# A megakernel of four stages: clearing a finished stage's semaphores on SyncE inside the next stage, and the sum and two norms ahead of the latent attention as one block

## The chip, the cores and the metric

One core of one Trainium2 chip runs the whole program. The metric is the device time of one execution in microseconds, taken as the median of several runs. A profiled execution gives the trace on which the working rests.

## What is computed

The input is x, 2048 tokens of 128 features. Four residual sublayers follow each other, each closed by a layer norm without weights:

```python
x = _layernorm(x + mamba_block(x))             # state space, 4 heads
x = _layernorm(x + local_transformer(x))       # two layers: 8 heads, window 64, gated feed-forward
x = _layernorm(x + latent_attention(x))        # 16 heads; begins with a layer norm of its own input
x = _layernorm(x + experts(x))                 # 16 experts, 4 per token, and a shared one

def _layernorm(x, axis=-1, eps=1e-05):
    m = jnp.mean(x, axis=axis, keepdims=True)
    v = jnp.var(x, axis=axis, keepdims=True)
    return (x - m) / jnp.sqrt(v + eps)
```

The latent attention starts with `h = (x - mu) * rsqrt(var + eps) * ln_scale + ln_bias`, so between the local transformer and the latent attention a sum and two norms stand in a row: `x + y`, the norm of the sublayer, and the norm of its result without the weights (the weights are put on after the transposes).

## The kernel before

The tokens lie in 16 tiles of 128 (T = 16), the partitions hold the tokens of a tile and the free dimension the 128 features; four tiles make a chunk of 512 (NC = 4). x_tok and y_tok are two such arrays of [128, 16, 128] that stay in SBUF through the whole kernel, in float32.

The program is a row of blocks (`nc.Block()`). In a block each engine has its own list of instructions, and the engines are ordered among each other by semaphores; at a block's end all engines meet at a barrier. Between two blocks nothing overlaps. `Space` (L34) holds the tiles and the semaphores of a stage, and notes every semaphore it hands out in `Space.used`. Semaphores count upwards, so one must be back at zero before its number is used anew. `clear_semaphores` (L63) does that: a block of its own in which GpSimd clears every used semaphore one by one (L70), after which they are released. It is called four times: after the state space and its two norms (L522; 49 semaphores), after each of the two layers of the local transformer (L1198; 56 and 55), and after the latent attention and its norm n2 (L1792; 64).

`normalise` (L76) is a block: for each of 16 tiles the vector engine takes statistics (L93) and aggregates them (L96); ScalarE takes the root of all 16 variances at once (L128), the vector engine inverts it (L101) and normalises tile by tile (L105). The last output of it is needed by the next block.

The local transformer (L1168) begins with a small block in which SyncE issues four loads: the weights wqkv and rows of layer 0 (L539, L540), the mask band (L1183) and the rotation tables turns (2 MB, L1184). The vector engine waits for band, casts it, and with that the block ends. Then each layer (`attention_layer`, L543) runs three blocks: the projections (`project_qkv`, L555), the windowed attention and the feed-forward. In the projections' block SyncE loads wo (L593) and waits for it. TensorE transposes the tokens in four groups (L603), projects q, k (L614) and v (L618) tile by tile, and transposes the rotated result (L630); ScalarE copies one half of each transposed group (L650) and squares q and k (L656); the vector engine copies the other half (L695), rotates (L703, L711) and sums the squares (L718); GpSimd first scales the rotation tables (L749, it needs turns) and then adds (L756) and scales (L762) each tile. TensorE takes up the first two groups, then tile 0, group 2, tile 1 and group 3, in this order.

After layer 1 and its clearing a block with a single instruction adds the two arrays (L1203, 2048 columns), then come `normalise` n1 (L1204) and, inside `latent_attention` (L1221), `normalise` gn (L1232), which writes to the other array. The next block (ga, L1245) issues its loads of weights, transposes and projects. The main part of the latent attention is a loop of four turns over heads and chunks; the change does not touch it. The experts' first block (L1833) issues seven loads on SyncE (L1838, L1840).

## Time and profile before

| | |
|---|---|
| median of 3 runs | 2432.08 us (2427.37 to 2432.56) |
| the profiled execution | 2424.45 us |
| its span | 2422.6 us |
| TensorE busy | 2123.5 us (88%) |
| TensorE weight loads busy | 1305.8 us (54%) |
| vector engine busy | 1629.8 us (67%) |
| ScalarE busy | 1383.3 us (57%) |
| GpSimd busy | 900.5 us (37%) |
| DMA moved | 345.62 MB |

The profile is of one execution. A busy TensorE counts the time in which a matmul is under way, whatever the clock; the clock granted to it is shown beside it, where 1.00 is 2.4 GHz and 0.50 is 1.2 GHz. Names ending in q (SPq, POOLq) are the instructions that an engine's queue carries out itself: issuing a DMA, setting, waiting for or clearing semaphores, and draining at a barrier. They are not counted as busy. SP is SyncE, POOL is GpSimd, DVE is the vector engine, ACT is ScalarE, PE is TensorE, PEld its weight loads. A row of the timeline gives the start, the duration, the engine and line, the operation with output<-input, the shapes, how many instructions were merged, and in brackets how long the engine had been idle and what released it. Times of the trace count from the start of the span.

### The profile page before, as it was taken

Reading aid. Unit: us, or ns where it says so; the run is one execution under the profiler, and the core shown is the slowest. Engines: PE = TensorE matmul, PEld = TensorE weight load, DVE = VectorE, ACT = ScalarE, POOL = GpSimd, SP = SyncE. Lnnn points to the kernel's source line nnn. Section 1 sums busy time; section 2 is a strip of 40 time slices with the busy share of each in tenths; the row PEclk is TensorE's granted clock in tenths of the full one; section 3 lists DMA queues with packets and bytes.
Section 4 is the critical chain, followed back from the end, with each engine's and each line's share of the span. In section 5 each row is a group of like instructions: output and inputs, shape, how many; then the busy total and the mean of one; then the engine's idle time right before and its main releaser. Section 6 shows DMA issues by size and latency. Waiting matters only on the chain. (4 is left out here: it accounts for less than half of the span.)

```text
span 2422.6 us, 38119 instructions
## 1 busy us (share of the span) xinstructions
PE 2123.5 (88%) x11662; PEld 1305.8 (54%) x11662; DVE 1629.8 (67%) x3035; ACT 1383.3 (57%) x2804; POOL 900.5 (37%) x889
## 2 busy tenths in 40 slices
PE   4745898889964799999999999999999999996497
PEld 2533486547742455555555555555555555553254
DVE  5767765576655677777677776777776777773544
ACT  4333665366520477777677776777776777773121
POOL 0635632474302334444344343443434434442000
PEclk8887899989986799999999999999999999998598
DMA  1001000000004476767677676677766776673100
GB/s 32 1 1 58 1 2 27 5 1 2 2 12 153 132 235 231 242 230 240 207 232 241 231 239 232 218 232 238 231 231 219 239 232 233 228 242 123 36 1 18
DMA packets 224395, 345.62 MB, mean 143 GB/s; under 512 B 16992, under 2 KB 169696, under 8 KB 223904
## 3 DMA queue, kind: packets, MB, share of 16 engines
q1 hardware_dynamic: 224160, 342.86, 42.9%
q8 instruction: 102, 1.67, 0.3%
q14 instruction: 133, 1.09, 0.1%
HBM read 148.55 MB, written 136.31 MB: 118 GB/s over the span
## 5 line engine op out<-in xcount | busy, mean ns | idle before, releaser
L1503 DVE TENSOR_REDUCE g.most<-g_score 128x1 f32<-128x512 f32 x1028 | 639.5, 684 | 350.5 <-PE g_score L1473 347.9
L1511 ACT ACTIVATE g.probs<-g_score,g.bias 128x1024 f32<-128x1024 f32 x514 | 568.6, 1111 | 67.1 <-DVE g.bias L1506 55.7
L1473 PE MATMUL g_score<-g.keys,g.q_unit 128*128 128x512 f32 x2056 | 561.2, 413 | 25.4 <-DMA g.q_unit<-g.q_pair 11.8
L1496 ACT ACTIVATE g.near<-g_turned 128x512 f32<-128x512 f32 x512 | 305.4, 597 | 322.1 <-PE g_turned L1492 322.1
L1473 PEld LDWEIGHTS g_score<-g.keys,g.q_unit 128*128 128x128 f32 x2056 | 360.7, 190 | 145.0 <-ACT g.probs L1511 61.8
L1492 PEld LDWEIGHTS g_turned<-top.ident,g.probs 128*128 128x128 f32 x2048 | 234.1, 140 | 243.0 <-issue 208.1
L1570 DVE STREAM_TRANSPOSE g.blocks<-g.probs 128x1024 f32<-128x1024 f32 x256 | 318.9, 1246 | 23.9 <-DMA bounce<-g.blocks 16.2
L1492 PE MATMUL g_turned<-top.ident,g.probs 128*128 128x128 f32 x2048 | 321.6, 279 | 0.0
L1524 PE MATMUL g_mix_ps<-g.near,mid.y_tok 128*64 128x512 f32 x1056 | 258.7, 611 | 6.6 <-DMA g.far<-bounce 6.6
L1524 PE MATMUL g_mix_ps<-g.far,mid.y_tok 128*64 128x512 f32 x1056 | 255.2, 605 | 0.0
L1590 POOL TENSOR_TENSOR mid.y_tok<-mid.y_tok,g.waves 128x512 f32<-128x512 f32 x128 | 164.3, 1284 | 231.9 <-ACT mid.y_tok L1488 231.9
L1552 POOL TENSOR_TENSOR g.scaled<-g.scaled,g.recip 128x512 f32<-128x512 f32 x67 | 69.8, 1042 | 425.9 <-ACT g.scaled L1544 414.8
L1524 PEld LDWEIGHTS g_mix_ps<-g.near,mid.y_tok 128*64 128x64 f32 x1056 | 64.9, 137 | 104.9 <-issue 97.0
L1524 PEld LDWEIGHTS g_mix_ps<-g.far,mid.y_tok 128*64 128x64 f32 x1056 | 64.3, 136 | 99.5 <-issue 99.5
L1511 ACT ACTIVATION_READ_ACCUMULATOR g.probs<-g_score,g.bias 128x1 f32 x514 | 100.5, 195 | 0.0
L1601 POOL TENSOR_TENSOR g.k_part<-mid.y_tok,g.zero 128x256 fp32r<-128x256 f32 x64 | 39.3, 613 | 155.9 <-DMA g.keys<-g.k_part 150.7
L1593 POOL TENSOR_TENSOR mid.y_tok<-mid.y_tok 128x256 f32<-128x256 f32 x128 | 93.5, 730 | 10.0
L1556 POOL TENSOR_TENSOR top.x_tok<-top.x_tok,g.scaled 128x512 f32<-128x512 f32 x67 | 85.8, 1280 | 5.2
L1488 ACT ACTIVATE mid.y_tok<-g_side 128x512 f32<-128x512 f32 x128 | 77.4, 605 | 2.0
L881 POOL TENSOR_TENSOR lt0.probs<-lt0.probs,lt0.total 128x768 f32<-128x768 f32 x32 | 47.0, 1468 | 71.3 <-DVE lt0.total L936 71.3
L881 POOL TENSOR_TENSOR lt1.probs<-lt1.probs,lt1.total 128x768 f32<-128x768 f32 x32 | 47.0, 1468 | 71.2 <-DVE lt1.total L936 71.2
L1349 PE MATMUL g_side<-g.c,g.w_up 64*128 64x256 f32 x512 | 72.6, 402 | 0.0
(362 smaller groups left out, 3184.9 us busy)
## 6 DMA issues: line engine op xcount, KB each, us to landing
bounce<-g.blocks SPq DMA_DIRECT2D x256, 512.0 KB, 5.2
g.far<-bounce SPq DMA_DIRECT2D x256, 512.0 KB, 4.4
g.q_unit<-g.q_pair SPq DMA_DIRECT2D x132, 256.0 KB, 4.7
g.keys<-g.k_part SPq DMA_DIRECT2D x256, 64.0 KB, 3.5
g.far<-g.near SPq DMA_DIRECT2D x8, 512.0 KB, 5.8
lt.turns<-turns SPq DMA_DIRECT2D x1, 2048.0 KB, 9.1
g.waves<-g_waves SPq DMA_DIRECT2D x1, 2048.0 KB, 10.2
g.keys<-g.probs SPq DMA_DIRECT2D x16, 128.0 KB, 2.3
```

The lines of the kernel that those rows point to most:

```text
L881: nc.gpsimd.tensor_tensor(p, p, total[:, slot].unsqueeze(2).broadcast_to([P, HH, KEYS]), ALU.mult).then_inc(m["probs_ready"], 1)
L1473: ins = nc.tensor.matmul(score[:, b], q[:, part], k_of(b), start=(part == 0), stop=(part == 1))
L1488: nc.scalar.activation(raw[:, kind], side[:, kind], ACT.Copy).then_inc(m["piece_taken"], 1)
L1492: ins = nc.tensor.transpose(turned[:, k * P:(k + 1) * P], probs[:, r % 2, t * P:(t + 1) * P], ident[:])
L1496: nc.scalar.activation(near[:, w, tiles, r * P:(r + 1) * P], turned[:].rearrange("p (t n) -> p t n", n=P), ACT.Copy).then_inc(m["near_copi ...
L1503: nc.vector.tensor_reduce(most[:, slot, k:k + 1], score[:, k], AX.X, ALU.max, negate=True)\
L1511: nc.scalar.activation(probs[:, slot, k * 2 * CH:(k + 1) * 2 * CH], score[:, 2 * k:2 * k + 2].rearrange("p b n -> p (b n)"), ACT.Exp, bias ...
L1524: ins = nc.tensor.matmul(out, values[:, t], moving, start=(t < 2), stop=(t >= T - 2))
L1556: nc.gpsimd.tensor_tensor(a, a, scaled[:], ALU.add).then_inc(m["added"], 1)
L1570: nc.vector.transpose(blocks[:, r % 2].rearrange("p j t c -> p t j c"), probs[:, r % 2, NEAR * P:].rearrange("p (t j a) -> p t j a", j=4, ...
L1590: nc.gpsimd.tensor_tensor(both, both, waves[:, at].rearrange("p s n -> p (s n)"), ALU.mult)\
L1593: nc.gpsimd.tensor_tensor(total, total, both[:, QH:], ALU.add).then_inc(m["order"], 1)
```

## The change

`clear_semaphores` is gone. `retire_semaphores` only sets the used semaphores aside, with no instruction; `clear_retired` clears them on SyncE, one by one, in a block of the next stage:

- the 49 of the state space in the first block of the local transformer, between the loads of wqkv and rows and the loads of band and turns;
- the 56 of layer 0 in the projections' block of layer 1, between the load of wo and the wait for it;
- the 55 of layer 1 in the new block with the sum and the two norms, where SyncE has nothing else to do;
- those of the latent attention in the experts' first block, behind its seven loads.

The sum, n1 and gn become one block, `normalise_twice`. The sum is cut in four pieces of 512 columns. Statistics, aggregation, root and reciprocal are as before. The mean of a normalised tile is taken as zero and its variance as var / (var + eps), which two multiplications of the 16 variances give (`left`); ScalarE takes a second root, and the vector engine inverts it between its fourth and fifth tile (`again`). The vector engine normalises each tile in place, and ScalarE multiplies each by its value of `again` and writes it to the other array. The array cur takes the second norm, x the first, as before.

```diff
--- before.py
+++ after.py
@@ -35,7 +35,7 @@
-    used = []
+    used, retired = [], []
     def __init__(self, nc, name):
         self.nc, self.name, self.stack = nc, name, ExitStack()
@@ -60,17 +60,17 @@
         return sem
-def clear_semaphores(nc):
-    with nc.Block() as block:
-        @block.gpsimd
-        def _(pool):
-            for _, sem in Space.used:
-                pool.sem_clear(sem)
-    while Space.used:
-        Space.used.pop()[0].__exit__(None, None, None)
+def retire_semaphores():
+    Space.retired, Space.used = Space.used, []
+def clear_retired(sync):
+    for _, sem in Space.retired:
+        sync.sem_clear(sem)
+    while Space.retired:
+        Space.retired.pop()[0].__exit__(None, None, None)
 def normalise(nc, name, src, dst, scale=None, shift=None, residual=None):
@@ -131,6 +131,65 @@
+def normalise_twice(nc, x, cur, after):
+    with Space(nc, "n1") as sp:
+        stats = sp.sb("stats", [P, T, 6])
+        moments = sp.sb("moments", [P, T, 2])
+        spread = sp.sb("spread", [P, T])
+        again = sp.sb("again", [P, T])
+        left = sp.sb("left", [P, T])
+        eps = sp.sb("eps", [P, 1])
+        names = ["eps_ready", "summed", "stats_ready", "std_ready", "order", "left_ready", "left_std", "again_ready",
+                 "once"]
+        m = {n: sp.sem(n) for n in names}
+        with nc.Block() as block:
+            @block.sync
+            def _(sync):
+                after(sync)
+            @block.vector
+            def _(dve):
+                nc.vector.memset(eps[:], EPS).then_inc(m["eps_ready"], 1)
+                for g in range(NC):
+                    tiles = slice(4 * g, 4 * g + 4)
+                    nc.vector.tensor_tensor(x[:, tiles], x[:, tiles], cur[:, tiles], ALU.add).then_inc(m["summed"], 1)
+                for t in range(T):
+                    dve.wait_ge(m["summed"], t // 4 + 1)
+                    nc.vector.bn_stats(stats[:, t], x[:, t]).then_inc(m["order"], 1)
+                for t in range(T):
+                    dve.wait_ge(m["order"], t + 1)
+                    ins = nc.vector.bn_aggr(moments[:, t], stats[:, t])
+                ins.then_inc(m["stats_ready"], 1)
+                dve.wait_ge(m["std_ready"], 1)
+                link = Chain(dve, m["order"])
+                link.n = T
+                link(nc.vector.reciprocal(spread[:], spread[:]))
+                dve.wait_ge(m["stats_ready"], 1)
+                link(nc.vector.tensor_tensor(left[:], moments[:, :, 1], spread[:], ALU.mult))
+                nc.vector.tensor_tensor(left[:], left[:], spread[:], ALU.mult).then_inc(m["left_ready"], 1)
+                for t in range(T):
+                    if t == 4:
+                        dve.wait_ge(m["left_std"], 1)
+                        nc.vector.reciprocal(again[:], again[:]).then_inc(m["again_ready"], 1)
+                    nc.vector.tensor_scalar(x[:, t], x[:, t], moments[:, t, 0:1], spread[:, t:t + 1],
+                                            ALU.subtract, ALU.mult).then_inc(m["once"], 1)
+            @block.scalar
+            def _(act):
+                act.wait_ge(m["eps_ready"], 1)
+                act.wait_ge(m["stats_ready"], 1)
+                nc.scalar.activation(spread[:], moments[:, :, 1], ACT.Sqrt, bias=eps[:, 0:1])\
+                    .then_inc(m["std_ready"], 1)
+                act.wait_ge(m["left_ready"], 1)
+                nc.scalar.activation(again[:], left[:], ACT.Sqrt, bias=eps[:, 0:1]).then_inc(m["left_std"], 1)
+                act.wait_ge(m["again_ready"], 1)
+                for t in range(T):
+                    act.wait_ge(m["once"], t + 1)
+                    nc.scalar.activation(cur[:, t], x[:, t], ACT.Copy, scale=again[:, t:t + 1])
 HEADS_S, HEAD_S, STATE = 4, 64, 128
 INNER = HEADS_S * HEAD_S
 TAPS = 4
@@ -519,7 +578,7 @@
         normalise(nc, "ssn", out_tok, out_tok, ln_w, ln_b, x_tok)
     normalise(nc, "n0", out_tok, out_tok)
-    clear_semaphores(nc)
+    retire_semaphores()
@@ -591,6 +650,8 @@
             @block.sync
             def _(sync):
                 sync.dma_start(wo[:], dram[f"wo{layer}"]).then_inc(m["wo_loaded"], 16)
+                if layer:
+                    clear_retired(sync)
                 sync.wait_ge(m["wo_loaded"], 16)
             @block.tensor
@@ -1180,6 +1241,7 @@
                 @block.sync
                 def _(sync):
                     load_projection(sync, dram, tables, 0)
+                    clear_retired(sync)
                     sync.dma_start(band32[:], dram["band"]).then_inc(got, 16)
                     sync.dma_start(tables["turns"][:], dram["turns"]).then_inc(tables["loaded"], 16)
@@ -1195,13 +1257,8 @@
                     nc.vector.tensor_copy(tables["band"][:], band32[:])
         for layer in range(DEPTH):
             attention_layer(nc, dram, const, tables, layer, x if layer == 0 else cur, cur)
-            clear_semaphores(nc)
-        with nc.Block() as block:
-            @block.vector
-            def _(dve):
-                nc.vector.tensor_tensor(x[:], x[:], cur[:], ALU.add)
-    normalise(nc, "n1", x, x)
+            retire_semaphores()
+        normalise_twice(nc, x, cur, after=clear_retired)
@@ -1229,7 +1286,6 @@
         waves = sp.sb("waves", [P, HALVES, 2, QH])
         mixers = sp.sb("mixers", [P, 2 + HEADS_G, D])
         waves_loaded = sp.sem("waves_loaded")
-        normalise(nc, "gn", x, acc)
         with Space(nc, "ga") as s:
             norm = s.sb("norm", [P, 2])
             w_down = s.sb("w_down", [P, 2 * LATENT])
@@ -1789,7 +1845,7 @@
                 take_output(act, UNITS + 2)
     normalise(nc, "n2", acc, x)
-    clear_semaphores(nc)
+    retire_semaphores()
@@ -1838,6 +1894,7 @@
                         sync.dma_start(d[:], dram[n]).then_inc(m["loaded"], 16)
                     for d, n in ((w_gate, "w_gate"), (w_up, "w_up_e"), (w_down, "w_down_e")):
                         sync.dma_start(d[:], dram[n]).then_inc(w_loaded, 16)
+                    clear_retired(sync)
                 @block.tensor
                 def _(pe):
```

## Rows read from the trace of the kernel before

**Rows 1.** The timeline around the sum and the two norms: start us, us, engine line operation

```profile
710.66 0.29 DVE L1142 TENSOR_TENSOR top.x_tok<-top.x_tok,fp_prod 128x128 f32<-128x128 f32 x1 [0.38 <-PE fp_prod L1054]
...
715.04 2.29 DVE L1203 TENSOR_TENSOR mid.y_tok<-mid.y_tok,top.x_tok 128x2048 f32<-128x2048 f32 x1 [4.09 <-PEq L65]
...
717.67 3.19 DVE L93 BATCH_NORM_STATS2 n1.stats<-mid.y_tok 128x6 f32<-128x128 f32 x16
...
723.65 0.25 DVE L101 RECIPROCAL n1.spread<-n1.spread 128x16 f32<-128x16 f32 x1 [1.72 <-ACT n1.spread L128]
...
737.94 1.94 PE L1259 MATMUL ga_turned<-top.ident,top.x_tok 128*128 128x128 f32 x8 [27.32 <-PEq L87]
```

**Rows 2.** The timeline around the first joint, after the state space

```profile
188.67 4.19 DVE L105 TENSOR_SCALAR mid.y_tok<-mid.y_tok,n0.moments,n0.spread 128x128 f32<-128x128 f32 x16
...
196.51 0.33 SPq L539 DMA_DIRECT2D lt.wqkv<-wqkv  x1
...
197.36 0.42 SPq L1183 DMA_DIRECT2D lc.band<-band  x1
...
202.59 1.94 PE L603 MATMUL lp_turned<-top.ident,mid.y_tok 128*128 128x128 f32 x8 [33.74 <-PEq L1178]
...
207.00 9.30 POOL L749 TENSOR_TENSOR lp0.turns<-lt.turns,lt.rows 128x1024 f32<-128x1024 f32 x4 [10.02 <-DMA lt.turns<-turns]
```

**Rows 3.** The timeline around the joint of layer 0 and layer 1

```profile
454.56 0.29 DVE L1142 TENSOR_TENSOR top.x_tok<-top.x_tok,fp_prod 128x128 f32<-128x128 f32 x1 [0.38 <-PE fp_prod L1054]
...
459.30 1.94 PE L603 MATMUL lp_turned<-top.ident,top.x_tok 128*128 128x128 f32 x8 [4.78 <-PEq L65]
...
460.42 0.70 DVE L695 COPY lp1.hT<-lp_turned 64x512 f32<-64x512 f32 x1 [0.85 <-PE lp_turned L603]
...
465.18 0.60 PE L603 MATMUL lp_turned<-top.ident,top.x_tok 128*128 128x128 f32 x4
...
467.34 1.22 DVE L703 TENSOR_TENSOR lp1.rotated<-lp_qk_ps,lp1.turns 128x1024 f32<-128x1024 f32 x1 [0.76 <-ACT lp1.square L656]
```

**Rows 4.** The timeline around the joint before the experts

```profile
2237.43 4.19 DVE L105 TENSOR_SCALAR mid.y_tok<-top.x_tok,n2.moments,n2.spread 128x128 f32<-128x128 f32 x16
...
2246.23 0.36 SPq L1838 DMA_DIRECT2D ea.router<-router  x1
```

**Rows 5.** Queue instructions of one line: count, ns min/median/max, first and last start us

```profile
L70 POOLq EVENT_SEMAPHORE_RANGE_CLEAR  x49: 37/38/47, 193.1 to 196.2; - x49
...
L65 POOLq EVENT_SEMAPHORE  x8: 17/17/17, 196.3 to 2246.1; - x8
...
L65 SPq EVENT_SEMAPHORE  x4: 17/17/17, 196.4 to 2246.2; - x4
```

**Rows 6.** Timeline, then stretches with TensorE's granted clock (ahead of the DMA share)

```profile
222.92 1.88 PE L614 MATMUL lp_qk_ps<-lt.wqkv,lp0.hT 128*128 128x512 f32 x4
...
408.77 0.67 PE L1026 MATMUL fp_prod<-top.x_tok,lt.moved 128*128 128x256 f32 x2 [0.65 <-PEq L801]
...
408.20:408.75 0.55, 0.00 (x0) 0.01 (x1) 0.25 (x1) 0.02 (x1) 0.01 (x1) 1.00 0.00 0
...
459.20:460.30 1.10, 1.00 (x5) 1.03 (x6) 0.17 (x2) 0.00 (x0) 0.95 (x1) 0.50 0.13 15
```

**Rows 7.** Transfers by issue: count, KB each, us from issue to landing

```profile
la1.wo<-wo SPq DMA_DIRECT2D x1, 256.0 KB, 2.5
...
lc.band<-band SPq DMA_DIRECT2D x1, 192.0 KB, 4.5
```

**Rows 8.** ScalarE's groups of one shape: count | busy us, mean ns | idle before

```profile
L670 ACT ACTIVATE la0.qkT<-lp_turned 128x512 f32<-128x512 f32 x32 | 17.2, 594 | 5.1 <-PE lp_turned L630 5.1
...
L1097 ACT ACTIVATE ff0.gelu<-fp_g_ps,ff0.b 128x512 f32<-128x512 f32 x12 | 8.2, 687 | 23.4 <-PE fp_g_ps L1044 23.4
...
L216 ACT ACTIVATE ss.xbc<-ss.xbc,ss.conv_b 128x2048 f32<-128x2048 f32 x4 | 8.0, 2001 | 14.9 <-DVE ss.xbc L245 14.9
...
L495 ACT ACTIVATE ssd.square<-ss.gate 128x256 f32<-128x256 f32 x16 | 6.7, 416 | 9.1 <-PEq L341 8.7
```

## The prediction

> **What bounds the kernel now.** Read the page from its fourth part first. The chain that ended last is of little use here: it is followed back only through the last norm and stops at a barrier, so its shares of the span are all next to nothing. So the question is not which engine is the bottleneck of the whole span, but what happens on the few stretches that the change touches. These are the joints between stages, so the next view is the timeline around each joint, with the engines' queues: the work on both sides of a joint is serial (a barrier of all engines stands between two blocks), and whatever is taken out of a joint is taken out of the time, unless something that starts with the next block is late anyway.
>
> There are two kinds of joint. A plain one, such as the end of the sum on the vector engine (715.04 + 2.29 = 717.33) to the first statistics at 717.67, costs 0.33 us [rows 1]. One with clearing is long: 188.67 + 4.19 = 192.86 to 196.51 is 3.65 us [rows 2]; 454.85 to 459.30 is 4.45 [rows 3]; 710.95 to 715.04 is 4.09 [rows 1]; 2241.62 to 2246.23 is 4.61 [rows 4]. The row of the clearing line names the cause [rows 5]: 49 clears on GpSimd's queue, the last one 3.1 us after the first, so 64 ns apart though each is 38 ns long. The lists of the other three joints are, counted in the code, 56, 55 and 64 long, and at 64 ns they fill those gaps too. During a clear all other engines wait at the barrier.
>
> **The change, part by part.**
>
> *Layer 0 to layer 1 of the local transformer (56 clears).* The clears go to SyncE behind the load of wo in the first block of layer 1. That block lasts from 459 to past 531, SyncE has nothing else in it, so 56 x 64 ns = 3.6 us are covered; without that cover they would cost themselves. Joint: 4.45 - 0.33 = 4.1 us saved. There is more. The row of the window from 459.2 shows TensorE's granted clock at 0.50 (1.2 GHz) after 4.8 us of idle; the joint at 408.2, where the engine had been idle for 0.65 us, shows 1.00 (2.4 GHz) [rows 6]. With the clears gone the idle time at this joint is about 0.7 us, close to the second case, so I take it that layer 1 starts at 2.4 GHz. What it is worth: before, the third group of transposes starts at 465.18, 5.9 us after the block's first one, and this releases ScalarE's square and then the vector engine's first rotation at 467.34 [rows 3]. At full clock four transposes take 0.6 (half of what 1.94 for eight gives, with the tail), the copy of 0.70 follows, then six matmuls (four for q and k, two for v) at 0.43 each, since four take 1.88 with their tail [rows 6]: 0.65 + 0.75 + 2.6 = 4.0 instead of 5.9. Then the vector engine is the limit of the block, tile after tile, so the 1.8 us stay. Late next is GpSimd, whose scaling of the turns (9.3 us for four pieces) stands before its first addition; but in layer 0 it started only at 207.00, 4.4 us after that block's first transposes, and the block was hardly longer. Sum: **5.9**, bounds 4.1 (clock falls all the same) and 6.3.
>
> *State space to local transformer (49 clears).* Here the clears stand in SyncE's queue between the loads of wqkv and rows and the loads of band and turns. The block opens 3.65 - 0.33 = 3.3 earlier, at 193.2. SyncE needs 197.36 - 196.51 = 0.85 for the two loads ahead [rows 2], then 49 clears. No row shows a clear on SyncE. From above: a DMA issue, 0.42 long and with the same gap 0.45 apart [rows 2]. From below: a semaphore event takes 17 ns on SyncE and 17 ns on GpSimd [rows 5], so the engines are alike there, and with the gap of 26 ns between instructions 43 ns is the floor. The nearest row is the same instruction on GpSimd, so I take 64: 3.1 us, and band is issued at 193.2 + 0.85 + 3.1 = 197.2 instead of 197.36. Nearly the whole gain is eaten by the new place. What is left comes from the transfer: band landed 4.5 us after its issue, behind 0.9 MB of wqkv and rows issued at the same moment; wo of layer 1, larger than band and alone, took 2.5 [rows 7]. With wqkv under way 3.3 us earlier I take 2.7 for band. The vector engine's cast and the barrier are unchanged, so the block after it starts (4.5 - 2.7) + 0.17 = **2.0** earlier. Late next: turns (2 MB), issued right behind band, on which GpSimd waits until 207.00 [rows 2]; they come some 1.5 earlier, and GpSimd had slack there as well. Bounds: 0.2 (landing still takes 4.5) and 3.4 (clears at 43 ns, landing in 2.3); far below zero at the price of a DMA issue, see the rivals. TensorE starts cold here both ways.
>
> *Layer 1, the sum and two norms.* Before: 710.95 (end of the last add) to 737.94 (first transposes of the latent attention), 27.0 us [rows 1]. After: the 55 clears run on SyncE beside the norm, 3.5 us within some 16, and are covered. The block opens at 711.28. The sum in four pieces costs what one did, 2.29, plus the start of three instructions, from 0 to 3 x 0.19 (one of sixteen statistics in 3.19); 0.15 taken: 713.7. From the first statistics to the first reciprocal nothing changes, 723.65 - 717.67 = 6.0 (it contains ScalarE's table load): 719.7. Then come that reciprocal, 0.25, and two small multiplications, at most as long each: 720.5 with rounding up. Sixteen tiles take 4.19 in every norm [rows 2], four of them 1.05: 721.55, then the second reciprocal, 0.3 with its signal: 721.85. The second root on ScalarE runs under the first four tiles. From here ScalarE copies sixteen tiles of 128 columns with a scale read from a column. Its price comes from four rows [rows 8]: 256 columns from SBUF take 0.416, 2048 with a column operand 2.001; a column operand costs 0.687 - 0.594 = 0.093 at 512 columns; so a column of width costs (2.001 - 0.093 - 0.416) / 1792 = 0.83 ns, and a tile 0.416 - 0.107 + 0.093 = 0.40. Back to back they overlap: 32 of 0.594 are busy for only 17.2, in pairs, so 0.11 are hidden. At 0.30 apart, 15 x 0.30 + 0.40 = 4.9: 726.75. The vector engine is done at 725.0, so ScalarE ends the block. With 0.3 of barrier the next one starts at 727.05 instead of 737.94: **10.9**. Bounds 10.3 (no overlap of the small ones, more start cost) and 12.5 (ScalarE keeps up with the vector engine). No work is moved behind the joint: the loads of the latent attention are issued in the next block as before and shift with it.
>
> A rule of the Trainium skill bears on this: Perfetto Trace Analysis, Optimizing Scalar/DVE Operations, advises larger operations, as each has a fixed cost, and gives about 93 ns for ScalarE on SBUF. By it, as an estimate, a tile would come every 0.2 us, ScalarE would stay just behind the vector engine, and this part would give 12.5 instead of 10.9; the same rule speaks against cutting the sum in four, at about 0.06 us for each start. The trace does not bear out the 93 ns as the whole price here: a column operand alone adds as much again [rows 8].
>
> *Latent attention to experts (64 clears before; they go behind the seven loads of a block of some 43 us).* 4.61 - 0.33 = **4.3**. TensorE had long been idle and starts cold both ways. Bounds 4.1 and 4.4.
>
> **The sum.** 2.0 + 5.9 + 10.9 + 4.3 = 23.1 us. The profiled execution took 2424.45 (span 2422.6 and 1.85 around it), so a profile of the changed kernel should read 2401.3. The median of the runs shown is 2432.08, 7.6 above the profiled one and itself in a spread of 5.2; the loop of the latent attention, some 1400 us, is not touched. I predict 2432.1 - 23.1 = **2409.0**.
>
> **The rivals.**
>
> *The clock falls all the same* in layer 1's first block. For it: the granted clock there was 0.50, and I argue from one short joint. Against: that joint. It gives 23.1 - 1.8 = 21.3, so 2410.8.
>
> *ScalarE keeps up* with the vector engine in the joined norm. For it: plain copies without a column operand come 0.2 apart. Against: the 0.093 of a column operand [rows 8]. It gives 24.7, so 2407.4. This is the result of the rule of the Trainium skill cited above, and has the same chance.
>
> *A clear on SyncE is dear.* This is the case on the slow side. SyncE's other work is DMA issues at 0.45 us each; if a clear cost p, the joints would give together 26.2 - 49 p for p up to 0.28 (at 0.064 that is the sum above), and beyond that 55 clears also outlast the 15.5 us of the joined norm, which costs a further 55 (p - 0.28). The gain is zero at p = 0.40; at 0.45 it is 26.2 - 22.0 - 9.4 = -5.2, so 2437. Against: semaphore events take 17 ns on both engines [rows 5].
>
> *The gain is real but other stretches move.* Every cold start of TensorE and the phase of the transfers in the long loop shift by chance; four iterations of that loop at 0.5 us each, and the runs' spread, could take away or add up to 8: 2401 to 2417. Here also falls that the code of a new stage was loaded under the clears: the joint with 56 clears is 0.3 longer than the others' spacing gives.
>
> **Chances.** Forecast 0.62; clock falls 0.11; ScalarE keeps up 0.10; other stretches move 0.13, of which 0.02 hide the gain altogether; dear clears 0.04, of which 0.03 are slower. The range runs from 2401 (all upper bounds, 26.6, and 4.5 of spread) to 2416 (all lower bounds, 18.7, and 2.6), and leaves out less than 2 in 10. A difference of 0.2%, 4.9 us, is about what a measurement of this kernel can tell from none. Faster 0.94, same 0.03, slower 0.03.
>
> **What would show it.** In the changed profile: the clearing rows under SyncE with their spacing (43 to 64 ns right, 400 wrong); the vector engine's gaps at the three other joints near 0.33; the first window of layer 1 at clock 1.00 and the first rotation about 6.2 us after the block's first transpose (8.0 before); band landing some 2.7 us after its issue; ScalarE's sixteen copies 0.30 apart and ending 1.5 us or more after the vector engine's last tile; and some 16 us from the first piece of the sum to the first transpose of the latent attention (22.9 before). The prediction is wrong if SyncE's clears are slow, if band lands as late as before, or if the long loop takes another time than before.

## The result

| | before | after |
|---|---|---|
| median | 2432.32 us (2427.37 to 2433.67, 4 runs) | 2403.61 us (2399.72 to 2404.37, 4 runs) |
| profiled execution | 2424.45 us | 2404.37 us |
| its span | 2422.6 us | 2402.6 us |

After stands to before as 0.9884 (95% interval 0.9867 to 0.9901): 28.7 us faster, between 24.1 and 32.3. The forecast was 2409.0 with a range from 2401 to 2416, so the time fell into the range, 5.4 us below the forecast.

The two profiled executions differ by only 20.0 us. The stretch that makes the difference is the loop of the latent attention, which the change does not touch: measured from the first issue of w_up to the first statistics of n2, it took 1469.5 us in the profile of before and 1475.1 in that of after. Over the 13 traces of this study it took from 1468.6 to 1479.4, and three traces of the kernel before alone read 1469.5, 1475.9 and 1477.2. So here the traces are compared outside that loop, joint by joint: the time outside it is 953.1, 954.2 and 951.5 us in three traces of before, and 927.5 and 929.9 in two of after (the second is the run after_again, below). That is a difference of 24.2 between the means.

The timeline of after at the first joint (start us, us, engine line operation, then the idle time before it and what released it; [rows 2] is its counterpart; the row of L105 is still n0's sixteen tiles):

```profile
189.12 4.19 DVE L105 TENSOR_SCALAR mid.y_tok<-mid.y_tok,n0.moments,n0.spread 128x128 f32<-128x128 f32 x16
...
193.57 0.33 SPq L598 DMA_DIRECT2D lt.wqkv<-wqkv  x1
...
197.79 0.33 SPq L1245 DMA_DIRECT2D lc.band<-band  x1
...
200.81 1.94 PE L664 MATMUL lp_turned<-top.ident,mid.y_tok 128*128 128x128 f32 x8 [31.51 <-PEq L1239]
...
207.68 9.29 POOL L810 TENSOR_TENSOR lp0.turns<-lt.turns,lt.rows 128x1024 f32<-128x1024 f32 x4 [13.63 <-DMA lt.turns<-turns]
...
210.13 1.22 DVE L764 TENSOR_TENSOR lp0.rotated<-lp_qk_ps,lp0.turns 128x1024 f32<-128x1024 f32 x1 [2.22 <-POOL lp0.turns L810]
```

The block opens early (wqkv at 193.57, 0.26 after the norm's end at 193.31; 3.65 before), band is issued 4.5 us after the norm's end, exactly as before, and the first transposes come 7.50 after it instead of 9.73. But the last row is new: the vector engine waits 2.22 us for GpSimd's scaled turns, which begin at 207.68.

The clearing rows of after, by stretch (count: ns min/median/max, first and last start; [rows 5] is the counterpart):

```profile
L71 SPq EVENT_SEMAPHORE_RANGE_CLEAR  x49: 25/30/49, 194.4 to 197.7; - x49
...
L71 SPq EVENT_SEMAPHORE_RANGE_CLEAR  x56: 25/28/30, 454.9 to 458.1; - x56
...
L71 SPq EVENT_SEMAPHORE_RANGE_CLEAR  x55: 25/30/31, 704.9 to 708.5; - x55
...
L71 SPq EVENT_SEMAPHORE_RANGE_CLEAR  x61: 25/25/46, 2232.1 to 2236.0; - x61
```

A clear on SyncE takes 25 to 30 ns, less than GpSimd's 38, yet they come 58 to 69 ns apart (3.3 us over 48 steps in the first row): nearly GpSimd's spacing. So the time of the instruction does not set the spacing; no run shows what does.

The joint of layer 0 and layer 1, timeline of after ([rows 3]):

```profile
454.62 1.06 PE L664 MATMUL lp_turned<-top.ident,top.x_tok 128*128 128x128 f32 x8 [0.65 <-PEq L1059]
...
458.78 0.60 PE L664 MATMUL lp_turned<-top.ident,top.x_tok 128*128 128x128 f32 x4
...
460.95 1.23 DVE L764 TENSOR_TENSOR lp1.rotated<-lp_qk_ps,lp1.turns 128x1024 f32<-128x1024 f32 x1 [0.76 <-ACT lp1.square L717]
```

and the window over its first transposes (window, length, busy time of PE, PEld, DVE, ACT, POOL with their counts, granted clock, DMA share, GB/s; [rows 6]):

```profile
454.60:455.70 1.10, 1.06 (x8) 0.85 (x8) 0.58 (x3) 0.41 (x1) 1.03 (x1) 1.00 0.32 26
```

TensorE was idle for 0.65 us instead of 4.78, the clock stayed at 1.00 (2.4 GHz), eight transposes took 1.06 instead of 1.94, and the first rotation comes 6.3 us after the first transpose instead of 8.0.

The joined norm, timeline of after ([rows 1]; ahead of it the last addition of the block before, then the sum, the reciprocals, the two outputs and the next block):

```profile
704.36 0.29 DVE L1203 TENSOR_TENSOR top.x_tok<-top.x_tok,fp_prod 128x128 f32<-128x128 f32 x1 [0.39 <-PE fp_prod L1115]
...
705.00 2.50 DVE L157 TENSOR_TENSOR mid.y_tok<-mid.y_tok,top.x_tok 128x512 f32<-128x512 f32 x4
...
713.38 0.25 DVE L168 RECIPROCAL n1.spread<-n1.spread 128x16 f32<-128x16 f32 x1 [1.71 <-ACT n1.spread L183]
713.67 0.17 DVE L170 TENSOR_TENSOR n1.left<-n1.moments,n1.spread 128x16 f32<-128x16 f32 x1
713.88 0.17 DVE L171 TENSOR_TENSOR n1.left<-n1.left,n1.spread 128x16 f32<-128x16 f32 x1
...
715.16 3.08 DVE L176 TENSOR_SCALAR mid.y_tok<-mid.y_tok,n1.moments,n1.spread 128x128 f32<-128x128 f32 x12
715.28 4.78 ACT L190 ACTIVATE top.x_tok<-mid.y_tok,n1.again 128x128 f32<-128x128 f32 x16 [0.88 <-DVE n1.again L175]
...
720.35 1.94 PE L1315 MATMUL ga_turned<-top.ident,top.x_tok 128*128 128x128 f32 x8 [16.02 <-PEq L146]
725.26 1.53 DVE L1344 TENSOR_SCALAR ga.hT<-ga_turned,ga.norm 128x512 f32<-128x512 f32 x2 [7.02 <-DMA ga.w_o<-w_o]
```

From the end of the last addition to the first transposes of the latent attention it is now 720.35 - 704.65 = 15.70 us, 26.99 before. The vector engine has its last tile at 718.24, ScalarE its last copy at 720.06: ScalarE ends the block, by 1.8 us. The last row is a wait that the prediction does not name: the vector engine of the next block stands until 725.26, 4.9 us after the first transposes, for the weights. It stood there before as well (6.0 us after them).

The joint before the experts ([rows 4]):

```profile
2224.19 4.19 DVE L105 TENSOR_SCALAR mid.y_tok<-top.x_tok,n2.moments,n2.spread 128x128 f32<-128x128 f32 x16
2228.64 0.95 POOL L1931 MEMSET ea.comb<- 128x1024 f32 x1 [11.26 <-POOLq L87]
2228.64 0.36 SPq L1894 DMA_DIRECT2D ea.router<-router  x1
```

2228.38 to 2228.64 is 0.26, where it was 4.61.

### The profile page after: what moved, and what is told of

Read it like the earlier page. It is cut to its first block and busy times, and to the rows that moved or that the text cites. A ratio compares the mean times of both kernels' runs of the same rounds, so it can differ in the third digit from the quotient of the medians.

```text
span 2402.6 us, 38021 instructions
## 1 busy us (share of the span) xinstructions
PE 2121.2 (88%) x11662; PEld 1305.6 (54%) x11662; DVE 1621.9 (68%) x2991; ACT 1388.2 (58%) x2820; POOL 898.4 (37%) x889
## 5 line engine op out<-in xcount | busy, mean ns | idle before, releaser
L1626 DVE STREAM_TRANSPOSE g.blocks<-g.probs 128x1024 f32<-128x1024 f32 x256 | 318.9, 1246 | 34.0 <-DMA bounce<-g.blocks 24.2
L1592 PE MATMUL g_side<-g.mixers,g.mixed 128*128 (+1 forms) x536 | 71.8, 277 | 1.2 <-ACT g.mixed L1588 1.2
```

What stands on the lines that cost most here:

```text
L1626: nc.vector.transpose(blocks[:, r % 2].rearrange("p j t c -> p t j c"), probs[:, r % 2, NEAR * P:].rearrange("p (t j a) -> p t j a", j=4, ...
```

## The experiments

**The change once more, and its two halves.** Four kernels ran on one chip beside the kernel before (median 2430.66 us, 2423.31 to 2433.49, 11 runs). The changed kernel, unedited:

> The changed kernel once more, beside the kernel before on one chip. By the joints (the theory): the stretches outside the latent attention's loop are the same as in the first trace of it within 1 us, and give 22 to 26 us together against the kernel before; the loop alone differs from trace to trace by several us with no change in it. If that holds, the measured gain is 23 to 29 us. The rival, that the change makes the loop itself faster, expects a loop shorter than the 1469.5 us of before in most traces and a gain of 28 us or more.

2403.09 us (2399.20 to 2406.40), 0.9891 (0.9873 to 0.9909): the result holds in a second set of runs, 27.6 us faster. Its loop took 1469.7 us, so the rival's shorter loop is not seen. Outside the loop the two traces of the changed kernel differ by 2.4 us, not by less than the 1 us expected; the experts' first block alone took 2.4 us longer in this one.

Only the clears move; sum, n1 and gn stay three blocks, and the 55 clears of layer 1 stand in the block of the sum:

```
-        normalise_twice(nc, x, cur, after=clear_retired)
+        with nc.Block() as block:
...
+            def _(sync):
+                clear_retired(sync)
...
+            def _(dve):
+                nc.vector.tensor_tensor(x[:], x[:], cur[:], ALU.add)
+    normalise(nc, "n1", x, x)
...
+        normalise(nc, "gn", x, acc)
```

> Only the clears are moved to SyncE; the sum, n1 and gn stay three blocks, and layer 1's clears run on SyncE in the block of the sum. The theory: 1.0 us from the first joint (nearly all eaten by the clears that stand before band and turns), 5.8 from the joint of the two layers, 4.3 before the experts, and 3.8 less about 1.4 at the sum, because 55 clears of 65 ns last 3.6 us and the sum only 2.3, so that SyncE ends that block. Together 13.5 us, 2418.8 if the kernel before takes 2432.3. The rival, that clears hidden beside work cost nothing anywhere, expects 15 us or more and a sum block of 2.3.

2415.37 us, 0.9934 (0.9917 to 0.9950), 15.3 us faster. Its trace has 4.35 at the experts' joint and 5.8 at the second joint, as the whole change has, and at the joint ahead of the sum 3.8, of which 1.6 are lost again: the clears run from 705.0 to 708.7 and outlast the sum (705.07 + 2.29 = 707.36). The time alone would fit the rival too, which asked for 15 us or more; the block of the sum, held open by the clears, refutes it.

Only the norms are joined, the clears stay on GpSimd in blocks of their own:

```
-    retire_semaphores()
+    clear_semaphores(nc)
...
-        normalise_twice(nc, x, cur, after=clear_retired)
+        normalise_twice(nc, x, cur, after=lambda sync: None)
```

> Only the sum and the two norms are joined in one block; the four clearing blocks stay on GpSimd. The theory: the span from the first piece of the sum to the first transpose of the latent attention is 15.4 us instead of 22.9, so 7.5 us, with up to 1 us more behind it from the landing of the next weights: 2424 to 2425. With clears_only it adds up to the whole change within the spread, apart from the 1.4 us at the sum that the joined block covers. The rival, that the gain is one of either part and the other is hidden, expects one of the two kernels at the level of before.

2420.45 us, 0.9958 (0.9942 to 0.9974), 10.2 us faster. In its trace the stretch from the first piece of the sum to the transposes is 731.00 - 715.64 = 15.36, against 22.90 before: 7.5. By their traces the first half is worth 0.6 (what is left of the first joint, below) + 5.8 + 2.2 + 4.35 = 12.9 and the second 7.5; both are timed 2 to 3 us better, within their intervals (6.3 to 14.1 us for the second). 15.3 + 10.2 = 25.5 against 27.6 for the whole: within the spread of the times the halves add. The traces show the one interaction that was expected: 12.9 + 7.5 = 20.4 against 22.1 for the joints of the whole, because the 1.6 us by which the clears outlast the sum are covered in the joined block.

**The first joint: where the clears stand.** One edit puts the 49 clears behind the loads of band and turns:

```
                     load_projection(sync, dram, tables, 0)
-                    clear_retired(sync)
                     sync.dma_start(band32[:], dram["band"]).then_inc(got, 16)
                     sync.dma_start(tables["turns"][:], dram["turns"]).then_inc(tables["loaded"], 16)
+                    clear_retired(sync)
```

> The changed kernel with one edit: in the first block of the local transformer the 49 clears stand behind the loads of band and turns instead of before them. The theory (clears in SyncE's queue hold back turns, and turns holds back GpSimd and the first rotation of layer 0): band is issued 3.3 us earlier and lands 4.5 us after its issue again, the next block starts about 1.2 us earlier, turns lands 3.2 us earlier, and the first rotation no longer waits for GpSimd; together 2 to 3 us faster than the changed kernel, about 2401. The rival, that turns take their time for another reason (their 2 MB alone), expects the first rotation unchanged and 1 us or less.

2401.93 us, 0.9887 (0.9870 to 0.9904). Its timeline:

```profile
193.89 0.42 SPq L1244 DMA_DIRECT2D lc.band<-band  x1
...
198.96 1.94 PE L664 MATMUL lp_turned<-top.ident,mid.y_tok 128*128 128x128 f32 x8 [30.18 <-PEq L1239]
...
203.78 9.30 POOL L810 TENSOR_TENSOR lp0.turns<-lt.turns,lt.rows 128x1024 f32<-128x1024 f32 x4 [10.26 <-DMA lt.turns<-turns]
```

The norm ends at 192.79 here, so band is issued 1.10 after it (4.5 in after) and the transposes start 6.17 after it (7.50). Band now lands 4.4 us after its issue, as before the change, since wqkv travels beside it again. The joint is worth 3.6 us instead of 2.2, and the block's last rotation starts at 265.04, 72.25 after the norm, where it is 74.97 in after and 75.71 in before. The trace says 2.7 us better than after; the timed difference to the changed kernel on that chip, 1.2, cannot confirm it, for each median moves by as much.

The other edit makes the clearing there twice as long, `for _, sem in Space.retired: sync.sem_clear(sem)` ahead of `clear_retired(sync)` (this one and the next three ran once each, on one chip, where the kernel before took 2422.84 in its one run; single times say little here, since runs of one kernel lie up to 15 us apart, so only their traces are used):

> The changed kernel with the 49 clears of the first joint issued twice, ahead of band and turns. Theory (each clear in front of a load on SyncE costs its spacing of 65 to 70 ns in full): band is issued 3.2 to 3.4 us later, the next block starts as much later, and so does layer 1. Rival (the loads have slack): the start of layer 1 moves by less than 1 us.

2411.11 us. Band is issued at 202.11, 7.3 us after the norm's end at 194.83 (4.5 in after), and the transposes follow at 205.23, 10.4 after it (7.50): 49 clears more put both 2.8 to 2.9 later (3.2 to 3.4 was expected). The price of a clear at this place is that of its spacing, 57 ns in the second pass, and all of it lies on the path.

**The first joint: where the gain of 2.2 us went.** Theory: GpSimd, which must scale all four chunks of the turns (9.3 us) before it adds and scales the first tile, is the late one. The edit loads the 2 MB of turns in four pieces, each with its own semaphore, and leaves the clears where the change has them:

```
-                    sync.dma_start(tables["turns"][:], dram["turns"]).then_inc(tables["loaded"], 16)
+                    for g in range(NC):
+                        tiles = slice(4 * g, 4 * g + 4)
+                        sync.dma_start(tables["turns"][:, tiles], dram["turns"][:, tiles])\
+                            .then_inc(tables["pieces"][g], 16)
...
                 for g in range(NC):
...
+                    pool.wait_ge(tables["pieces"][g], 16)
```

> The changed kernel with the clears where they are, and turns loaded in four pieces of 512 KB, each with a semaphore of its own, so that GpSimd scales the first piece when it has landed. Theory (GpSimd, held back by turns, sets the end of layer 0's projections): GpSimd starts 3 to 4 us earlier, and the last rotation comes 64 to 66 us after the block's first transposes instead of 67.5. Rival (the front of the block is set by TensorE and the vector engine alone): the first rotation and the last one stay where they are, 67.5.

2396.06 us. Two timelines show the mechanism. First after_again, the changed kernel with the turns in one load:

```profile
204.22 9.30 POOL L810 TENSOR_TENSOR lp0.turns<-lt.turns,lt.rows 128x1024 f32<-128x1024 f32 x4 [12.10 <-DMA lt.turns<-turns]
...
219.20 1.22 PE L691 MATMUL lp_turned<-top.ident,lp0.rotated 128*128 128x128 f32 x8 [2.42 <-POOL lp0.rotated L823]
...
220.21 3.50 PE L675 MATMUL lp_qk_ps<-lt.wqkv,lp0.hT 128*128 128x512 f32 x4
...
224.79 1.23 DVE L764 TENSOR_TENSOR lp0.rotated<-lp_qk_ps,lp0.turns 128x1024 f32<-128x1024 f32 x1 [2.08 <-ACT lp0.square L717]
```

with three windows: in the wait, over the first of the transposes, and over the four matmuls behind them:

```profile
217.00:219.00 2.00, 0.00 (x0) 0.00 (x0) 1.97 (x5) 0.03 (x1) 2.00 (x2) 1.00 0.00 0
219.20:220.00 0.80, 0.80 (x7) 0.80 (x8) 0.80 (x2) 0.47 (x1) 0.80 (x1) 1.00 0.00 0
220.20:221.30 1.10, 1.10 (x3) 0.58 (x3) 1.10 (x4) 0.85 (x2) 1.10 (x1) 0.50 0.00 0
```

and the same rows with the turns in pieces:

```profile
201.23 9.28 POOL L810 TENSOR_TENSOR lp0.turns<-lt.turns,lt.rows 128x1024 f32<-128x1024 f32 x4 [9.12 <-DMA lt.turns<-turns]
...
217.29 1.09 PE L691 MATMUL lp_turned<-top.ident,lp0.rotated 128*128 128x128 f32 x8 [0.60 <-POOL lp0.rotated L823]
218.22 1.88 PE L675 MATMUL lp_qk_ps<-lt.wqkv,lp0.hT 128*128 128x512 f32 x4
```

TensorE's list is fixed: project tile 3, transpose the rotated tile 0, project tile 4. Tile 0 comes from GpSimd 14.9 us after it began on the turns (204.22 to 219.1), which is later than TensorE is through with tile 3, so TensorE stands for 2.42 us. Then comes the expensive part: its granted clock is 1.00 through the wait, but falls to 0.50 (1.2 GHz) 0.8 us after the transposes have begun, the four matmuls of tile 4 take 3.50 instead of 1.88, ScalarE's square of that tile is late, and the vector engine, which is the limit of this block, loses 2.08. With the pieces GpSimd starts 2.3 us after the block's first transposes instead of 5.2, TensorE stands for 0.60, the clock stays, and the vector engine has no such wait; the block's last rotation comes 65.4 us after its first transposes instead of 67.5, as the theory had it. The other traces fall on the same two sides. Where that idle time is 0.6 to 1.3 (seven traces: three of before, norms_only, late_clears, pieces_only, loads_ahead) the next four matmuls take 1.88. Where it is 2.4 to 2.5 (six traces) they take 2.95 to 3.52 in five, the clock falling 0.2 to 0.9 us after the transposes have begun, and the vector engine loses 2.1 to 2.2. In the sixth, that of the result above, the clock held, although TensorE had stood 2.58 us there some 10 us earlier as well (at 212.70); so the wait goes with the fall but does not settle it, and why it held stays open. There the turns were so late (9.4 us from issue to landing, 7.9 in after_again) that the vector engine waited for them itself, 2.22 against a usual 0.76, and 0.48 at tile 4, which comes to 1.9. In both forms the earlier start is nearly all given back.

The Trainium skill describes a step like this one (TensorE: Matmul & The Clock Gate, section HAM oscillation): in a matmul loop that waits for its data at every turn, the clock is lowered in the wait and the next turn starts at the lower clock. The trace agrees in the price, 3.50 us where 1.88 was needed behind 2.42 of idle, and differs in the moment: the clock fell only after the work had begun again.

**The second joint: is it the idle time that costs the clock?** The clearing of layer 0 goes back to GpSimd in a block of its own, but TensorE transposes the identity in it, 34 times, into a scratch tile:

```
+            @block.gpsimd
+            def _(pool):
+                for _, sem in Space.used:
+                    pool.sem_clear(sem)
+            @block.tensor
+            def _(pe):
+                for k in range(count):
+                    nc.tensor.transpose(scratch[:, k % 4 * P:(k % 4 + 1) * P], ident[:], ident[:])
```

> The changed kernel with the 56 clears between the two layers back on GpSimd in a block of their own, while TensorE makes 34 transposes that nothing reads. Theory (the clears at this joint cost their own time, and besides that the idle TensorE lost its clock for the next block): the joint is 4.3 to 4.5 us again, but layer 1's first block starts at granted clock 1.00 and its first rotation comes 6.3 us after its first transposes, as in the changed kernel and not 8.0 as before. Rival (those 1.7 us have another cause, such as the earlier start of GpSimd's work): 8.0.

2405.66 us. The joint of warm_joint:

```profile
456.60 3.90 PE L82 MATMUL wj_scratch<-top.ident 128*128 128x128 f32 x34 [0.65 <-PEq L1079]
...
460.80 1.07 PE L684 MATMUL lp_turned<-top.ident,top.x_tok 128*128 128x128 f32 x8 [0.30 <-PEq L72]
...
467.13 1.22 DVE L784 TENSOR_TENSOR lp1.rotated<-lp_qk_ps,lp1.turns 128x1024 f32<-128x1024 f32 x1 [0.76 <-ACT lp1.square L737]
```

and its window, then that of norms_only, which has the same joint with TensorE idle:

```profile
460.80:461.90 1.10, 1.06 (x8) 0.83 (x8) 0.60 (x3) 0.43 (x1) 1.05 (x1) 1.00 0.21 35
```

```profile
459.90:461.00 1.10, 1.10 (x6) 1.10 (x7) 0.17 (x3) 0.01 (x1) 1.09 (x1) 0.50 0.23 48
```

The joint is as long as before the change (4.5 us), yet the clock is 1.00 and the first rotation comes 6.3 us after the first transpose; with the idle joint of norms_only the clock is 0.50 and it takes 8.0. So 4.1 of the 5.8 us are the clears and 1.7 the clock.

**The joined norm: what a copy on ScalarE costs.** The copies lose the second norm's scale, which is left out (`nc.scalar.activation(cur[:, t], x[:, t], ACT.Copy)`):

> The changed kernel with the sixteen activations of the joined norm as plain copies, without the scale read from a column, so the second norm's factor is left out. Theory (a column operand costs 93 ns an instruction, and ScalarE ends the block because of it): sixteen copies take 3.3 instead of 4.8 us, they end 0.3 to 0.6 us after the vector engine's last tile, and the next block starts 1.4 us earlier after the sum. Rival (the spacing is set by the signal of each tile from the vector engine): still 4.8.

2402.15 us. Its two outputs and the next block:

```profile
714.63 3.07 DVE L176 TENSOR_SCALAR mid.y_tok<-mid.y_tok,n1.moments,n1.spread 128x128 f32<-128x128 f32 x12
714.74 3.30 ACT L190 ACTIVATE top.x_tok<-mid.y_tok 128x128 f32<-128x128 f32 x16 [0.88 <-DVE n1.again L175]
718.34 1.94 PE L1315 MATMUL ga_turned<-top.ident,top.x_tok 128*128 128x128 f32 x8 [14.54 <-PEq L146]
```

Sixteen copies take 3.30 instead of 4.78, one every 0.20 us instead of 0.29, and ScalarE ends 0.34 after the vector engine instead of 1.8. The column operand costs (4.78 - 3.30) / 16 = 93 ns for each tile; from the first piece of the sum to the next block it is 13.87 instead of 15.35.

The Trainium skill has this figure in another place than the one that the prediction cited: ScalarE: Activation LUTs, What ACT_TABLE_LOAD costs, gives an ACTIVATE as a fixed part with 0.83 ns for each column, some 93 ns for each operand read by pointer, and about 93 ns hidden between neighbours; by these figures, as an estimate, copies of 128 columns back to back come 0.29 us apart with the operand and 0.20 without, and the traces bear out both. The 93 ns of Perfetto Trace Analysis are not the whole price.

**The kernel before, once more.** To see what two copies of one kernel differ by, it ran under two names of its own beside 13 runs of itself (median 2430.41, 2425.41 to 2440.42):

> The kernel before, unchanged, for a second trace of it. Theory (the loop of the latent attention differs by chance between executions): everything outside the loop takes 951 to 955 us as in the first trace, 23 to 26 more than in the changed kernel, and the loop anything from 1468 to 1476. Rival (the change touches the loop): a loop at 1469.5 again or below.

> The kernel before once more, for a third trace. Theory: outside the loop 951 to 955 us, the loop anywhere from 1468 to 1476. Rival: a loop at 1469.5 again or below.

2430.22 us, 0.9995 (0.9980 to 1.0011), and 2430.57 in a single run. Their traces give the 1475.9 and 1477.2 us of the loop named above, the second 1.2 above the range expected; outside the loop they have 954.2 and 951.5, as expected. The rival, that the change touches the loop, is not borne out.

**A version with what was learnt.** The clears stand behind band and turns; turns come in pieces; the joined norm's block issues the weights and waves of the latent attention ahead of its own clears; and the vector engine, which is done first, makes the last four of ScalarE's tiles (OWN = 4):

```
+                for t in range(T - OWN, T):
+                    dve.wait_ge(m["once"], t + 1)
+                    nc.vector.tensor_scalar(cur[:, t], x[:, t], again[:, t:t + 1], None, ALU.mult)
...
+            def load_and_clear(sync):
+                for d, n in ((norm, "g_norm"), (w_down, "w_down"), (w_v, "w_v"), (w_o, "w_o")):
+                    sync.dma_start(d[:], dram[n]).then_inc(ga_loaded, 16)
+                sync.dma_start(waves[:], dram["g_waves"]).then_inc(waves_loaded, 16)
+                clear_retired(sync)
```

> A version built on what the runs so far showed. Against the changed kernel: the 49 clears stand behind band and turns, turns is loaded in four pieces, the joined norm stands in the latent attention and SyncE issues the four weight loads and waves in its block, ahead of the clears, and the vector engine takes the last four of the sixteen second multiplications. Theory: 3 us at the first joint and in layer 0, 0.8 to 1.0 at the end of the joined norm, and 3.5 to 4 in the block behind it, whose first vector instruction waited 4.9 to 5.3 us for the weights: 7 to 8 us together, 2395 to 2396, ratio to before about 0.985. Rival (the next block waits for something else anyway, such as the cold TensorE): 4 us or less together.

2396.21 us (2393.71 to 2399.13), 0.9858 (0.9842 to 0.9875): the lowest ratio to before of all that were run more than once, some 6 to 8 us below the changed kernel (0.9884 and 0.9891), though the intervals still touch. In its trace:

```profile
196.63 0.36 DVE L1266 CAST lt.band<-lc.band 128x384 bf16<-128x384 f32 x1 [5.44 <-DMA lc.band<-band]
...
L71 SPq EVENT_SEMAPHORE_RANGE_CLEAR  x49: 25/30/49, 194.7 to 198.0; - x49
...
198.31 1.94 PE L670 MATMUL lp_turned<-top.ident,mid.y_tok 128*128 128x128 f32 x8 [31.13 <-PEq L1245]
...
709.82 3.61 ACT L196 ACTIVATE top.x_tok<-mid.y_tok,n1.again 128x128 f32<-128x128 f32 x12 [0.88 <-DVE n1.again L178]
...
712.69 0.87 DVE L183 TENSOR_SCALAR top.x_tok<-mid.y_tok,n1.again 128x128 f32<-128x128 f32 x4
...
713.86 4.04 PE L1325 MATMUL ga_turned<-top.ident,top.x_tok 128*128 128x128 f32 x16 [14.99 <-PEq L149]
...
715.06 1.59 DVE L1354 TENSOR_SCALAR ga.hT<-ga_turned,ga.norm 128x512 f32<-128x512 f32 x2 [1.50 <-PE ga_turned L1325]
```

The two engines end the norm within 0.13 us of each other (713.43 and 713.56), which gives 1.0, and the vector engine's first instruction of the next block comes 1.2 us after the transposes, where it was 4.9 in after (720.35 to 725.26): the wait for the weights, which nothing hid before, is gone, and that block takes 18.8 us instead of 22.5 (from its first transposes to the first issue of w_up).

The first joint gave less than the 3 us expected: the last rotation of layer 0 comes 72.7 us after the norm, some 2.3 better than in the two traces of the changed kernel. Here the clears stand behind four issues of turns in place of one, end at 198.0 and so outlast the cast (196.63 + 0.36 = 196.99) by 1.0 us; the transposes start 7.12 us after the norm's end at 191.19, where late_clears had 6.17. So the two edits at this joint are in each other's way, and a place behind the loads is free only as long as the block lasts longer than the clears.

## Why the prediction was right, and where it was not

In us; first joint: the block's start, then what is left of it at the block's last rotation.

| step | predicted | measured in the traces |
|---|---|---|
| first joint, start of layer 0 | 2.0 | 2.2 |
| of it kept in layer 0 | 2.0 | 0.6 to 0.7 |
| layer 0 to layer 1, joint | 4.1 | 4.1 |
| its clock | 1.8 | 1.7 |
| sum and two norms, clears included | 10.9 | 11.3 |
| before the experts | 4.3 | 4.35 |
| sum | 23.1 | 22.1 |
| outside the long loop | | 24.2 |
| medians | 23.1 | 28.7 (24.1 to 32.3) |

**The first joint** was right in its mechanism and wrong in what follows. Clears of 64 ns were taken and 69 measured, a landing of band after 2.7 and 2.3 measured, which together made the 2.2; late_clears and twice_cleared show that the clears' place ahead of band costs what was worked out. The step that failed is "they come some 1.5 earlier, and GpSimd had slack there as well". The turns came 0.2 us later (after) and 1.3 earlier (after_again) by the norm's end, while the block started 2.2 earlier, so they were later by the block's own clock. And there was no slack: before the change TensorE already stood 0.7 to 1.2 us for GpSimd's first tile. [rows 2] has GpSimd's start; what was missing in the working was the sum from there, 9.3 + two additions of 2.3 + one scaling of 1.0, against the moment at which TensorE is through with tile 3.

**Layer 0 to layer 1** came out within 0.1 in each of its two terms, and the rival that the clock falls all the same is refuted: the window at 454.60 has 1.00, and warm_joint shows that it is the idle time that costs the clock, not the joint's length.

**The joined norm** was 0.4 better than worked out. The two small multiplications were bounded by a reciprocal and took 0.17 each, the rest of the terms stood: four additions 2.50 against 2.44, sixteen copies 4.78 against 4.9, 1.8 behind the vector engine against 1.5 or more. The rival that ScalarE keeps up falls with plain_copies: it would be true without the column operand.

**The joint before the experts** was as predicted. **Dear clears** are refuted by the clearing rows. The 0.3 us that the prediction puts down to code loaded under the 56 clears lie between the clears themselves: those stood 69 ns apart on GpSimd (3.8 us over 55 steps), the other three groups 63 to 65. No run tells why.

**Where the rest of 28.7 comes from.** The joints hold 22.1. Outside the loop two more are seen in the traces, in the first block of the latent attention (22.5 and 23.5 us from the first transposes to the first issue of w_up, against 23.7, 24.2 and 23.1 before) and in the first block of the experts (40.8 and 43.2, against 43.4, 43.1 and 43.0; 40.7 to 43.4 in all traces with the clears moved into it); both contain waits for weights and TensorE at either clock, and no run tells chance from effect there. The remaining 4.5 are smaller than what the loop moves by between traces of one kernel, and the interval of the ratio, 24.1 to 32.3, just includes the traces' 24.2. From profile to profile the error has the other sign: the sum gave 2401.3 and 2404.37 was measured, 3.1 more, because the loop took 5.6 us longer in the second profile than in the first. The term of the prediction that was meant for this, 8 us either way for other stretches, covers both. This part stays open, and so the time fell 5.4 us below the forecast for a reason that the prediction's sum does not hold; that it stayed inside the range is in part luck, and what speaks for the mechanism is the table by steps. One of the prediction's signs of being wrong, a loop that takes another time than before, did come true (1475.1 against 1469.5), but the kernel before alone moves by 7.7 between its three traces, so that sign could not tell anything.

## What to carry to other kernels

Work that is moved from a gap of its own into a queue is hidden only if nothing that others wait for stands behind it there, and only if the block lasts longer than it: 49 clears more ahead of the load of band cost 2.8 us, the 49 behind the loads cost nothing in late_clears, but 1.0 us in loads_ahead and 55 of them 1.6 in clears_only, where they outlasted the rest of the block. When a joint gets shorter, work out again for each engine of the next block when its first input is due, in the order of every engine's list; an engine that was late by a harmless 1 us can be late by 2.5, and if TensorE's clock falls on top of it, the loss grows: at tile 4 the vector engine waited 0.5 us in the one trace where the clock held and 2.1 to 2.2 in the five where it fell. And compare traces by stage before comparing medians: the joints' 22 us could be read within 1 us, while an untouched loop of 1470 us moved by up to 11.

## What the runs showed of the hardware

- Clearing a semaphore takes 25 to 30 ns (median) on SyncE and 38 on GpSimd, but SyncE clears one only every 55 to 69 ns and GpSimd every 63 to 69.
- At one place in layer 0's projections six traces have a TensorE wait of 2.4 to 2.5 us: in five the clock was still 1.00 through the wait and fell to 0.50 within 0.9 us after it, in one it held. In the seven traces with a wait of 0.6 to 1.3 us there it held.
- A TensorE idle for 4.8 us at a joint went on at 0.50; with 34 transposes that nothing reads in the same joint it went on at 1.00, and the first rotation came 6.3 us after the block's first transposes instead of 8.0.
- One load of 2 MB, issued at the same place in the same order, landed after 7.8 to 9.4 us in six traces of the changed kernel and its variants. In four pieces the first can be used 2.9 us earlier after the block's start (GpSimd began at 2.3 instead of 5.2), with the same bytes.
- A band of 192 KB lands after 2.3 to 2.4 us when the loads ahead of it were issued 3.8 us earlier or more, and after 4.3 to 4.6 when it is issued 0.5 us behind them.
